# When the mixture-of-experts stage forms its positions, and how its eight groups of experts are ordered on TensorE

## The reference

```python
topk_idx, topk_w = _router(x, router_w, e_bias)
...
pos = jnp.arange(T * K, dtype=jnp.int32) - group_start[e_sorted]
valid = pos < C
...
Xp = x[slots_token].reshape(E, C, d)
G = jnp.einsum('ecd,edi->eci', Xp, W_gate)
U = jnp.einsum('ecd,edi->eci', Xp, W_up)
Y = jnp.einsum('eci,eid->ecd', jax.nn.silu(G) * U, W_down)
Yf = Y.reshape(EC, d) * slots_w[:, None]
out = jnp.zeros((T, d), x.dtype).at[slots_token].add(Yf)
shared = jax.nn.silu(x @ shared_gate.T) * (x @ shared_up.T) @ shared_down.T
```

## Time and profile before

| | |
|---|---|
| time, 3 runs | 735.45 us median, 735.08 to 735.92 |
| profiled execution | 732.78 us, of it 731.0 us span |
| granted TensorE clock, mean over the span | 0.974 |
| PE busy | 643.4 us (88%) |
| DVE busy | 446.8 us (61%) |
| ACT busy | 382.1 us (52%) |
| loads in the span | 105.04 MB, mean 144 GB/s |

### The profile page before, as it was taken

One profiled execution on the slowest core, in us unless ns is written; L12 is line 12 of the kernel. 1 busy time (PEld: TensorE's weight loads), 2 busy tenths in 40 slices (PEclk: granted clock), 3 DMA queues, 4 the chain that ended last, 5 costly groups with the idle time before them and its releaser, 6 DMA issues.

```text
span 731.0 us, 14846 instructions
## 1 busy us (share of the span) xinstructions
PE 643.4 (88%) x5860; PEld 454.7 (62%) x5860; DVE 446.8 (61%) x581; ACT 382.1 (52%) x564; POOL 48.8 (7%) x72
## 2 busy tenths in 40 slices
PE   5699899899899898898898898898978988899447
PEld 4666577676676676776676776796546875642112
DVE  2977688698698688688688688453134854300001
ACT  2543576676675676676675775783125863110000
POOL 2430000000000000000000000000001310000000
PEclk9999999999999999999999999999998997999868
DMA  9902795224224224224224224205983051289991
GB/s 359 419 35 44 148 356 109 50 46 92 49 43 91 48 43 91 48 43 91 48 43 91 48 47 88 49 2 199 420 345 145 1 186 74 87 345 421 418 416 67
DMA packets 25106, 105.04 MB, mean 144 GB/s; under 512 B 3696, under 2 KB 6896, under 8 KB 19184
## 3 DMA queue, kind: packets, MB, share of 16 engines
q1 hardware_dynamic: 25072, 104.57, 44.3%
HBM read 77.29 MB, written 0.52 MB: 106 GB/s over the span
## 4 chain that ended last, share of the span: by engine, by line
PE 61%; DVE 17%; issue 8%; ACT 6%; DMA 4%; SPq 3%; POOL 1%; DVEq 0%; ACTq 0%
PE psO L985 7%; PE psO L993 6%; DVE arena L693 6%; PE psO L986 5%; PE psS L973 5%; PE psS L972 5%; PE psM L945 5%; DVE arena L711 5%; PE psO L1057 4%; DMA arena<-w_exp 3%; SPq L360 3%; PE psS L1199 3%; PE psO L909 2%; PE psO L931 2%; PE psO L933 2%
## 5 line engine op out<-in xcount | busy, mean ns | idle before, releaser
L711 DVE TENSOR_TENSOR arena<-arena 128x1024 bf16<-128x1024 f32 x128 | 156.7, 1224 | 79.8 <-ACT arena L513 78.1
L511 ACT ACTIVATE arena<-psS 128x1024 bf16<-128x1024 f32 x128 | 131.2, 1025 | 113.2 <-PE psS L973 112.9
L693 DVE TENSOR_REDUCE arena<-psM 128x2 f32<-128x1024 f32 x128 | 155.9, 1218 | 14.8 <-PE psM L945 14.8
L985 PE MATMUL psO<-arena 128*128 128x129 bf16 x1024 | 133.4, 220 | 7.6 <-ACT arena L504 7.2
L986 PE MATMUL psO<-arena 128*128 128x128 bf16 x1024 | 132.5, 220 | 0.0
L513 ACT ACTIVATE arena<-psS 128x1024 f32<-128x1024 f32 x128 | 130.6, 1021 | 0.0
L972 PE MATMUL psS<-arena 128*128 128x256 bf16 x512 | 120.8, 273 | 0.8 <-ACT arena L497 0.8
L973 PE MATMUL psS<-arena 65*128 65x256 bf16 x512 | 120.8, 273 | 0.0
L985 PEld LDWEIGHTS psO<-arena 128*128 128x128 bf16 x1024 | 98.0, 98 | 30.3 <-issue 20.7
L986 PEld LDWEIGHTS psO<-arena 128*128 128x128 bf16 x1024 | 99.4, 97 | 0.4
L993 PE MATMUL psO<-arena 128*128 128x129 bf16 x1024 | 79.4, 220 | 8.8 <-DVE arena L711 8.4
(11 more groups left out here) (188 smaller groups left out, 738.9 us busy)
## 6 DMA issues: line engine op xcount, KB each, us to landing
arena<-w_exp SPq DMA_DIRECT2D x32, 1024.0 KB, 16.4
arena<-arena SPq DMA_DIRECT2D x96, 256.0 KB, 3.7
arena<-w_exp SPq DMA_DIRECT2D x32, 512.0 KB, 17.4
arena<-w_pair SPq DMA_DIRECT2D x8, 1088.0 KB, 16.9
arena<-w_o SPq DMA_DIRECT2D x1, 4096.0 KB, 20.4
arena<-ctx SPq DMA_DIRECT2D x4, 512.0 KB, 13.6
arena<-rope SPq DMA_DIRECT2D x4, 512.0 KB, 14.5
arena<-w_shared_in SPq DMA_DIRECT2D x1, 2048.0 KB, 8.3
```

The costliest lines, as they stand in the source:

```text
L511: nc.scalar.activation(p_hi[:, s % 2, :], psS[s % 2][:, :], ACT.Exp).then_inc(s_phi, 1)
L693: nc.vector.reduce_max(maxes[:, :, st, c], psM[:, :].rearrange("p (j n) -> p j n", j=2), AX.X).then_inc(s_mfree, 1)
L711: nc.vector.tensor_tensor(p_lo[:, s % 2, :], p_f[:, s % 2, :], p_hi[:, s % 2, :], ALU.subtract).then_inc(s_plo, 1)
L985: mm(psC[:, st, :], ph, vx[:, GROUP * g + i, 0:CW], start=g == 0 and i == 0 and st == 0, stop=False, skip_group_check=True)
```

## The change

The positions (L1166 to L1168) are formed behind `shared_hidden(0)` alone. Parts 1 to 3 of the shared expert go between the first groups: part 1 behind `gate_up(0)`, part 2 behind `down(0)`, part 3 behind `gate_up(1)`. Each group's `hidden_back` and `down` stand behind its own `gate_up`, with `shared_out` of a part, or a `combine`, between `gate_up` and `hidden_back` from group 2 to group 6. The weights by slot are transposed behind group 1, into another accumulator. The load of expert 12 moves from ahead of the other late loads to behind the first eight of them. No arithmetic is added or removed.

```diff
@@ sync
-            sp.wait_ge(sh_mm, SH_EARLY)
-            load_whole(RING_MID + 1)
             for g in range((E - RING + GE - 1) // GE):
                 new = range(RING + GE * g, min(RING + GE * (g + 1), E))
                 sp.wait_ge(gu_mm, g + 1)
...
                 sp.wait_ge(y_mm, g + 1)
                 for k in new:
                     load_expert(k, down, ld_down)
+                if g == 0:
+                    sp.wait_ge(sh_mm, SH_FREES)
+                    load_whole(RING_MID + 1)
@@ scalar
-            for i in range(SH_EARLY):
-                shared_silu(i)
+            shared_silu(0)
             for c in range(DC):
                 act.wait_ge(xp_mm, c + 1)
...
-            group_silu(0)
-            for i in range(SH_EARLY, DC):
-                shared_silu(i)
-            act.wait_ge(owT_mm, 1)
-            nc.scalar.copy(owT.rearrange("p g t -> p (g t)"), psM[:, 0:TRIOS * T]).then_inc(owT_copied, 1)
-            for g in range(1, NG):
-                group_back(g - 1)
+            for g in range(NG):
                 group_silu(g)
-            group_back(NG - 1)
+                if g == 0:
+                    shared_silu(1)
+                elif g == 1:
+                    shared_silu(2)
+                    shared_silu(3)
+                group_back(g)
+                if g == 1:
+                    act.wait_ge(owT_mm, 1)
+                    nc.scalar.copy(owT.rearrange("p g t -> p (g t)"), psS[0][:, 0:TRIOS * T]).then_inc(owT_copied, 1)
@@ vector
                 if g == 0:
-                    for i in range(SH_EARLY, DC):
-                        shared_product(i)
-                if g and g % 3 == 0:
-                    summed(g // 3 - 1)
-            summed(TRIOS - 1)
+                    shared_product(1)
+                elif g == 1:
+                    shared_product(2)
+                    shared_product(3)
+                if g % 3 == 2 or g == NG - 1:
+                    summed(g // 3)
@@ tensor
-            for i in range(SH_EARLY):
-                shared_hidden(i)
+            shared_hidden(0)
             pe.wait_ge(sel_done, 1)
...
                 for c in range(DC):
-                    if c == DC - 1 and g:
-                        hidden_back(g - 1)
                     for j in range(GE):
...
-            gate_up(0)
-            for i in range(SH_EARLY, DC):
-                shared_hidden(i)
-            weights_by_slot()
-            for g in range(1, NG):
+            for g in range(NG):
                 gate_up(g)
-                if g % 3 == 1 and g > 1:
-                    combine(g // 3 - 1)
-                down(g - 1)
-                if g <= DC:
-                    shared_out(g - 1)
-            hidden_back(NG - 1)
-            down(NG - 1)
+                if g == 0:
+                    shared_hidden(1)
+                elif g == 1:
+                    shared_hidden(3)
+                elif g < 2 + DC:
+                    shared_out(g - 2)
+                elif g == 6:
+                    combine(1)
+                hidden_back(g)
+                if g == 3:
+                    combine(0)
+                down(g)
+                if g == 0:
+                    shared_hidden(2)
+                elif g == 1:
+                    weights_by_slot()
             combine(TRIOS - 1)
```

More of the change, by code:

```diff
@@ L49 @@
 QK_BUFS, SM_BUFS = 4, 5
-SH_EARLY = 3
+SH_FREES = 3
 XPW = E * CAP + SLOT - CAP
@@ L857, in shared_product @@
                 nc.vector.tensor_tensor(hs[:, i, :], sh_bank[i][:, T:2 * T], hs[:, i, :], ALU.mult).then_inc(sh_done, 1)
-            for i in range(SH_EARLY):
-                shared_product(i)
+            shared_product(0)
             def summed(trio):
@@ L1178, in weights_by_slot @@
                 pe.wait_ge(ow_done, 2 * TT)
+                pe.wait_ge(hT_copied, 2)
                 for trio in range(TRIOS):
@@ L1181, in weights_by_slot @@
                         o = T * trio + P * st
-                        last = nc.tensor.transpose(psM[:, o:o + P], ow[:, st, P * trio:P * trio + P], ident)
+                        last = nc.tensor.transpose(psS[0][:, o:o + P], ow[:, st, P * trio:P * trio + P], ident)
                 last.then_inc(owT_mm, 1)
@@ L1205, in hidden_back @@
                 wait(pe, hT_copied, g - 1)
+                if g == 2:
+                    pe.wait_ge(owT_copied, 1)
                 for c in range(FC):
@@ L1212, in down @@
                 pe.wait_ge(hT_copied, g + 1)
-                if g == 0:
-                    pe.wait_ge(owT_copied, 1)
                 wait(pe, y_copied, trio - 1)
```

## The result

The changed kernel took 730.73 us in the median (727.59 to 730.78, 5 runs) where the kernel before took 735.45 us. The ratio is 0.9916, with a 95% interval from 0.9889 to 0.9943: 6.2 us faster (4.2 to 8.2). The forecast was 3.7 us. A second measurement on another occasion gave 0.9922 (0.9901 to 0.9943). The mean over all 11 timed executions of the changed kernel is 729.7 us, and over the 71 of the kernel before (those of experiment 1 among them) 735.0 us: 5.3 us between them. This is the number that I explain. Part of the first 6.2 us is chance: the five executions of the kernel before that were timed beside it, one of 738.35 us among them, have a mean of 736.0.

What follows compares the result with a forecast made beforehand. The prediction took the end of the expert weight stream, plus PE's work behind it, as the bound. Its terms, -5.2 + 1.7 + 3.8 - 0.9 - 3.1 = -3.7 us, took 735.45 to 731.7 us, range 729.6 to 733.4.

Steps and rivals of the forecast that it cites:

- Step 1: Front of the expert stage: positions formed sooner, so the late weight stream starts earlier, -5.2 us.
- Step 2: Gather: PE nearly idle for 3.6 us before it, so its clock falls to half speed, +1.7 us.
- rival B: The clock does not fall in the gather: -5.4 us in all, 730.0 us; chance 0.22.
- Steps 3 and 4: Late weight stream: expert 12 joins the bound stretch, +3.8 us; a hole before the first down closes, -0.9 us.
- Step 5: Groups 3 to 7: weights arrive in time and PE's idling before groups 5 to 7 hides moved work, 0 us.
- Step 6: Tail from the last gate_up to the last down: combine(1), down(6) and hidden_back(6) leave it, -3.1 us.

Runs made afterwards that it cites:

- experiment 1: The kernel before, unchanged, timed and traced again: ratio 1.0001.
- experiment 2: Kernel before with early positions, shared parts 1 to 3 behind the first gate_up and expert 12 loaded later, groups in old order: +1.6 us, ratio 1.0020.
- experiment 3: Kernel before with only the new group order, each hidden_back and down behind its own gate_up, front and loads as before: -4.2 us, ratio 0.9940.
- experiment 6: Changed kernel with four throwaway matmuls of 256 columns between the positions and the gather: -5.4 us against the kernel before, ratio 0.9926.
- experiment 4: Changed kernel with expert 12's load put back ahead of the other late loads: 740.2 us, ratio 1.0077 to the kernel before.
- experiment 5: The changed kernel, unchanged, timed and traced again: -5.7 us against the kernel before, ratio 0.9922.
- experiment 11: Changed kernel with the last gate and up weights sent ahead and four throwaway matmuls before the last gate_up: -8.8 us against the kernel before, ratio 0.9877.
- experiment 7: Changed kernel with expert 12's weights left out but for 16 columns of each part: -9.3 us against the kernel before, ratio 0.9886.
- experiment 8: Changed kernel with ten throwaway matmuls of 256 columns before the last gate_up: -6.7 us against the kernel before, ratio 0.9912.
- experiment 10: Changed kernel with gate and up parts of experts 29 to 31 sent earlier and down(6) behind hidden_back(7): -8.2 us against the kernel before, ratio 0.9887.
- experiment 9: Changed kernel with throwaway matmuls, four ahead of the gather and ten ahead of the last gate_up: -7.7 us against the kernel before, ratio 0.9897.
- experiment 12: Changed kernel with the last gate and up weights sent ahead and fillers before the gather and last gate_up: -9.2 us against the kernel before, ratio 0.9872.

## Why the prediction was too small

The events of the stage in the two traces of each kernel and in those of experiments 2, 3 and 6, as distances (worked out from the rows above, from the earlier trace rows and from the same rows of the other traces; the first column starts at the first 128x512 matmuls of the stage, L1136 before and L1138 after):

| | to the first late load | to the last `gate_up` | to the last `down` | sum |
|---|---|---|---|---|
| before, first trace | 37.0 | 72.3 | 10.3 | 119.6 |
| before, again | 37.6 | 73.2 | 10.1 | 120.9 |
| after, first trace | 32.1 | 75.7 | 8.2 | 116.0 |
| after, again | 33.7 | 75.5 | 7.05 | 116.2 |
| after, gap filled (6) | 32.1 | 75.8 | 8.2 | 116.1 |
| front alone (2) | 33.5 | 78.7 | 10.6 | 122.85 |
| group order alone (3) | 37.3 | 72.0 | 7.05 | 116.3 |

On the mean of the two traces of each, the changed kernel gained 4.4 us ahead of the first late load, lost 2.8 up to the last `gate_up`, and gained 2.6 behind it: -4.1. By the prediction these are -3.5, +2.9 and -3.1.

*Step 1, the stream starts earlier, -5.2:* right. DVE's add followed its own work at once, and between the first traces the first late load moved by -4.9 us, although the matmuls at the start of the stage took 0.4 us more for their clock (9.27 us in L1138, before 8.88 in L1136).

*Step 2, the clock in the gather, +1.7:* this is the step that failed. As the prediction put it, the new gap "is thin work in the manner of the second row and longer, so I take 1.7", and it was added to the sum in full. The size was right where the clock fell: 3.4 us at 0.50, and 6.26 us for the gather instead of 4.57. Two other things in it were wrong. First, the fall does not come every time: of eight traces of kernels with the early positions and no filler ahead of the gather, four show it (experiments 2, 4, 5, 11; 6.26 or 6.27 us) and four don't (the first trace, 7, 8, 10; 4.57 us). Second, where it came, it hardly reached the end: in experiment 5 the gather lost 1.69 us and the last `down` 0.30, since the last `gate_up` gave back 1.1. By the table the whole stage took 116.2 us with the fall and 116.0 and 116.1 without it (experiment 6). So the term belonged in the sum with about 0.2 and not 1.7: the prediction had it pass to the end whole, with a tail of the same length behind every start. Where the end no longer hangs on the last `gate_up`, the fall does count, with 1.5 us (experiments 10 and 11); the times of experiments 9 and 12 could not settle it. With this term at 0 the sum is -5.4 us, rival B. That the means stand 5.3 apart, so near it, is partly luck, since the traced stages are only 4.1 apart.

*Steps 3 and 4, expert 12 and the hole, +3.8 and -0.9:* right. From the first late load to the last `gate_up` the traces show +2.8 on the mean of two (+3.4 between the first two), where +2.9 was expected; expert 12 by itself is 3.6 to 3.7 (experiment 7), and that a hole opens when the first `down` is late is shown by experiment 2.

*Step 5, everything in time, 0:* right. PE waited 0.33 us before group 5, 6.80 before group 6 and 5.21 before group 7.

*Step 6, the tail, -3.1:* the mechanism was right, and its size moves with the clock: -2.1 and -3.3 in the changed kernel's two traces against the first trace of before, -3.1 in experiment 3 against the mean of before's two, and 5.35 us instead of 8.19 or 7.05 when the clock is held up (experiment 9). I had allowed 0.1 for "may last a little longer"; the low clock lasted 5.8 us in the first trace, against 3.5 before.

The two halves alone are worth +1.6 and -4.2 us, together -2.6; the change has -5.3. The remaining 2.7 is near the 2.45 us by which the hole of the front alone (3.3 us, experiment 2) is larger than the one before (0.85), and which the group order closes.

What stays open: the traced stages explain -4.1 us and not all of -5.3. Both traced executions of the changed kernel (730.75 and 731.03) are among its slower ones, and the faster ones (727.6 to 729.4) were not traced. Their granted clock over the span is 0.976 to 0.979 instead of 0.972 to 0.974. The fourteen traces show one place where such executions can differ, ahead of the stage, in code that the change does not touch. In five of them the clock is 1.00 in the windows 20 to 40 us and 500 to 520 us, and the stage begins at 603.4 to 603.5 us; in the other nine it is 0.91 in both, and the stage begins at 604.6 to 605.5. The first trace of the kernel before is of the first kind, both traces of the changed kernel are of the second. An execution of the changed kernel that began the stage 1.6 us earlier would take 729.1 to 729.4 us, an estimate, and four of its executions lie from 729.05 to 729.36. So that part of the scatter is no gain of the change. Whether an untraced execution also gains more within the stage was not seen.

## What to carry to other kernels

When a kernel's end hangs on a stream of loads, price an edit by when the stream starts, whether it runs dry, how much it carries, and what follows its last byte. Read from one trace, the first three held to within a few tenths here on the mean of the traces; what follows the last byte was 0.5 us off, and 1.0 in one trace, by the clock. An early start that doesn't free the next buffers in time is worth nothing (+1.6 us alone), and the group order, which shortens what follows the last byte and closes a hole, is the surest part (-4.2 us alone; sending first what has the longest chain behind it brought 3 more). A delay by a low clock upstream should not be added to the sum without asking what it meets downstream: here a start 1.44 us later behind a wait met 3.4 us of the next low stretch instead of 5.8. And an execution's time should be split at the start of the stage before it is credited to the change: up to 2.1 us of the scatter here arise ahead of it.

## What the runs showed of the hardware

The fall of TensorE's clock behind a gap of one and the same shape (PE busy 0.88 us of 3.5) is not fixed: 1.00 throughout the gather in one execution, 0.73 on the mean in another of the same kernel, with 4.57 and 6.26 us for the same 16 instructions. The low level in the last `gate_up` ended at nearly the same time of the execution (718.4 and 718.6) although PE's work there began 1.44 us apart, after waits of 4.36 and 5.21 us; it had begun at 715.0 in the one, 0.7 us into the work, and at 711.8 in the other, in the wait. Ten throwaway matmuls in the wait kept the clock at 1.00 and took `gate_up(7)` from 5.3 or 6.5 us to 3.64. When the late loads started after a stretch without any load, their first 2.5 us ran at 170 GB/s, and the 72 us behind them at 417.
